# Router logits with stationary router weights in four column groups, and the loop over the later steps written out

## What is computed

```python
def moe(x, sh_gate, sh_up, sh_down, r_gate, r_up, r_down, router_w, router_b):
    shared = expert_ffn(x, sh_gate, sh_up, sh_down)
    logits = x @ router_w + router_b          # (512 tokens, 512 channels) @ (512, 7)
    probs = jax.nn.sigmoid(logits)
    scores, idx = jax.lax.top_k(probs, TOPK)  # TOPK = 2
    ...
```

## Time and profile before

| | us |
|---|---|
| median of 3 runs | 2123.5 |
| lowest and highest | 2117.49, 2135.06 |
| the profiled execution's own time | 2125.45 |
| its span, first to last instruction | 2123.7 |

### The profile page before, as it was taken

How to read it: one execution, slowest core, us unless ns; L and a number is a source line. 1 busy time by engine, 2 the same in 40 slices (tenths; PEclk the granted TensorE clock), 3 DMA queues, 4 the chain that set the end, 5 groups by cost and what they waited for, 6 DMA issues and landing times. The chain is left out here.

```text
span 2123.7 us, 27520 instructions
## 1 busy us (share of the span) xinstructions
PE 1885.2 (89%) x9226; PEld 1238.9 (58%) x9226; DVE 1377.2 (65%) x2196; ACT 994.7 (47%) x1736; POOL 786.7 (37%) x1057
## 2 busy tenths in 40 slices
PE   7878665998999899997999899898899999899895
PEld 3446443695458565695447555496446666588442
DVE  5766698574563799574664699577554499667411
ACT  1412774462322786363232698264142399355021
POOL 1146377441210276561120177372020157472201
PEclk9989755998999999998999999999899999899898
DMA  6337100000213185200213176210022257310683
GB/s 259 109 115 245 52 0 20 1 2 1 99 45 119 57 266 173 96 25 22 79 51 119 35 244 227 84 41 21 17 97 93 69 175 263 127 41 21 237 311 104
DMA packets 55072, 221.09 MB, mean 104 GB/s; under 512 B 6288, under 2 KB 6288, under 8 KB 46992
## 3 DMA queue, kind: packets, MB, share of 16 engines
q1 hardware_dynamic: 45776, 195.14, 26.5%
q0 software_dynamic: 5120, 16.78, 2.4%
q10 hardware_dynamic: 4032, 7.34, 0.9%
HBM read 179.65 MB, written 39.58 MB: 103 GB/s over the span
## 5 line engine op out<-in xcount | busy, mean ns | idle before, releaser
L1933 POOL TENSOR_TENSOR Y<-Y,HC 128x1024 f32<-128x1024 f32 x116 | 273.9, 2362 | 174.0 <-DVE HC L1336 173.4
L1325 DVE TENSOR_TENSOR_SCAN HS<-DA,ps 128x1024 f32<-128x1024 f32 x128 | 292.3, 2284 | 23.5 <-PE ps L742 13.0
L534 PE MATMUL ps<-ring,XNT 128*128 128x512 f32 x384 | 182.4, 633 | 21.0 <-issue 12.2
L1688 ACT ACTIVATE DA<-DL,AB,AN 128x511 f32<-128x511 f32 x256 | 193.8, 806 | 14.8 <-DVE HS L1325 13.5
L954 PE MATMUL ps<-ring,XBT 128*128 128x512 f32 x384 | 188.5, 597 | 0.0
L1801 ACT ACTIVATE PD<-ps,NMX 128x128 f32<-128x128 f32 (+3 forms) x256 | 135.1, 530 | 101.2 <-DVE NMX L1470 99.2
L1470 DVE TENSOR_REDUCE NMX<-ps 128x1 f32<-128x128 f32 (+3 forms) x256 | 124.3, 487 | 65.4 <-PE ps L805 65.1
L823 PE MATMUL ps<-V,PTD 128*128 128x33 f32 x1280 | 164.2, 262 | 0.0
L823 PEld LDWEIGHTS ps<-V,PTD 128*128 128x128 f32 x1280 | 162.6, 192 | 0.5 <-ACT PTD L839 0.5
L650 PE MATMUL ps<-XNH,tern 128*128 128x512 f32 x352 | 139.2, 396 | 9.8 <-DVE tern L1225 5.4
L534 PEld LDWEIGHTS ps<-ring,XNT 128*128 128x128 f32 x384 | 76.6, 204 | 117.4 <-issue 108.1
(11 more groups left out here) (248 smaller groups left out, 4026.0 us busy)
## 6 DMA issues: line engine op xcount, KB each, us to landing
ring<-experts_dram SPq DMA_DIRECT2D x48, 1024.0 KB, 5.1
tern<-tern_q SPq DMA_DIRECT2D x33, 768.0 KB, 4.2
ring<-experts_dram SPq DMA_DIRECT2D x48, 512.0 KB, 5.4
RAW<-tern_dram SPq DMA_DIRECT2D x22, 768.0 KB, 4.8
ring<-wqkv_dram SPq DMA_DIRECT2D x4, 3072.0 KB, 11.9
XB<-xg SPq DMA_DIRECT2D x42, 256.0 KB, 3.6
yg<-YB SPq DMA_DIRECT2D x42, 256.0 KB, 4.9
tern_q<-tern SPq DMA_DIRECT2D x11, 768.0 KB, 7.0
```

The source lines that it names most:

```text
L534: last = pe.matmul(ps[:, 2 + 3 * (i % 2) + part], XNT[:, k, tile(i)], wqkv[:, k, part * C:(part + 1) * C], start=(k == 0), stop=(k == NK - 1))
L1325: v.tensor_tensor_scan(HS[:, q].rearrange("p j t -> p (j t)"), DA[:, q].rearrange("p j t -> p (j t)"), ps[:, 2 * q:2 * q + 2].rearrange("p ...
L1688: s.activation(DA[:, u % 2, jj, 1:T], DL[:, j, 1:T], ACT.Exp, scale=AN[:, j * NS + n:j * NS + n + 1], bias=AB[:, j * NS + n:j * NS + n + 1 ...
L1933: p.tensor_tensor(y, y, HC[:, q], ALU.add).then_inc(c_y, 1)
```

## The change

The router's weights are padded from 8 to 32 columns and become the stationary operand: `pe_logit_parts` issues four products, one for each block of channels k, each with 512 tokens as moving columns, into partitions 32k to 32k + 31 of bank 7 (bank 5 in `finish`). It stands ahead of tile 0 in `pe_A` and ahead of everything in `pe_experts`. ScalarE copies the 128x512 bank to a new tile ZT as its first work of the step (`s_logit_parts`). `pe_logits`, at its old place ahead of tile 1, waits for that copy and issues four products with 128 tokens of ZT stationary and 8 columns of a constant `fold` (four stacked unit matrices) moving, which adds the four parts and turns the result. In `finish` this second product comes behind the four gate products. The loop over steps 1 to 3 becomes three calls of `step` in a row.

```diff
-                  ("wo1", NK * C), ("wr", NK * 8), ("ident", P), ("bdt", NK), ("dpar", NK),
+                  ("wo1", NK * C), ("wr", NK * 32), ("ident", P), ("fold", 8), ("bdt", NK), ("dpar", NK),
...
+    ZT = at("ZT", [P, T], F32, "keep", 24 * KB)
...
         def pe_A(pe, experts):
+            if experts:
+                pe_logit_parts(pe)
             for i in range(NT):
                 if i == 1 and experts:
                     pe_logits(pe)
...
+        def pe_logit_parts(pe):
+
+            for k in range(NK):
+                last = pe.matmul(ps[32 * k:32 * k + 32, r_bank()], wr[:, k], XET[:, k], start=True, stop=True,
+                                 skip_group_check=True)
+            last.then_inc(e_part, 1)
+
         def pe_logits(pe):
-            for i in range(NT):
-                for k in range(NK):
-                    last = pe.matmul(ps[:, r_bank(), 8 * i:8 * i + 8], XET[:, k, tile(i)], wr[:, k],
-                                     start=(k == 0), stop=(k == NK - 1))
+
+            pe.wait_ge(e_parts, 1)
+            for i in range(NT):
+                last = pe.matmul(ps[:, r_bank(), 8 * i:8 * i + 8], ZT[:, tile(i)], cst("fold"), start=True, stop=True)
             last.then_inc(e_logit, 1)
...
         def pe_experts(pe):
+            pe_logit_parts(pe)
+            pe_E_part(pe, 0, 0, 0, NK)
             pe_logits(pe)
-            pe_E_part(pe, 0, 0, 0, NK)
             pe_counts(pe)
...
+        def s_logit_parts(s):
+            s.wait_ge(e_part, 1)
+            s.copy(ZT[:], ps[:, r_bank()]).then_inc(e_parts, 1)
...
         def s_A(s, experts):
+            if experts:
+                s_logit_parts(s)
...
         def s_experts(s):
+            s_logit_parts(s)
             s_route(s)
...
         step(x_rows[1], None, False)
-        with nc.Fori(1, B) as b:
-            step(x_rows[bass.ds(b + 1, 1)].rearrange("o p i c -> (o p) i c"),
-                 out_rows[bass.ds(b - 1, 1)].rearrange("o p i c -> (o p) i c"), True)
+        for b in range(1, B):
+            step(x_rows[b + 1], out_rows[b - 1], True)
         finish()
...
-    pad8 = np.zeros((C, 8), np.float32)
+    pad8 = np.zeros((C, 32), np.float32)
...
+        "fold": np.tile(np.eye(32, 8, dtype=np.float32), (NK, 1)),
```

More of the change, by code:

```diff
@@ L430, in build @@
         e_zb = sem("e_zb")
+        e_part = sem("e_part")
+        e_parts = sem("e_parts")
         e_sig = sem("e_sig")
```

## The result

| | before | after |
|---|---|---|
| median | 2123.88 (20 runs) | 2115.26 (20 runs) |
| lowest and highest | 2116.73, 2135.06 | 2111.37, 2124.07 |
| the profiled execution's own time | 2125.45 | 2111.37 |
| its span | 2123.7 | 2109.2 |
| mean granted clock | 0.928 | 0.932 |

What follows compares the result with a forecast made beforehand. Taken to bound it: the loop's jumps, TensorE's dense products up to the second q/k tile, and half clock. 7.8 + 3.8 + 0.5 + 3.8 + 1.0 = 16.9 us off 2125.45 gave 2108.5, named 2108; range 2101 to 2118.

Steps and rivals of the forecast that it cites:

- within 1%: Whole kernel: the case that the time changes by less than 1%, 21 us; chance 0.76.
- main forecast: Whole kernel: 2108 us, own range 2103 to 2113; chance 0.55.
- narrower column groups: Part products: rival that groups run two at a time (about 2112 us) or one at a time (2118); chance 0.15 for both.
- a clock that falls all the same: Steps: rival that the clock still falls behind the short products and new idle, 2119.5 us; chance 0.1.
- The rows of a step: Start of each step: 2.3 us idle, parts about 1.9, second product 0.9, tile 2 19.6 us after the first part.
- new wait: TensorE before the counts in each step: the wait for the mask, covered before, now open, 1.1 us idle.
- No loop, 7.8 us: Starts of steps 2 and 3 and the last block: less TensorE idle without the loop, 7.8 us gained.
- steps' logits, 3.8 + 0.5 + 3.8 us: Steps 1, 2 and 3: tile 2 starts sooner with the new logits, by 3.8, 0.5 and 3.8 us.
- After the last step, +1.0 us (0 to 1.3): Block after the last step: counts 1.3 us earlier, of which 1.0 us taken as gain.
- the bound 0: Block after the last step: an earlier scatter may land no earlier, sharing queues with the weights; gain 0.
- Straight code fetched late: Inside steps 2 and 3: rival that TensorE waits for instructions, slower from five waits on, six 2131 us; chance 0.05.
- More than that: Whole kernel: rival that half-clock stretches fall well or the clock rises sooner, 22 us or more gained; chance 0.15.

Runs made afterwards that it cites:

- e6: The changed kernel with the four part products accumulated in one column group, so that nothing runs side by side: 2121.76 us, ratio 0.999 to the kernel before.
- e2: The kernel before with its loop written out as separate steps and the old logits kept: 2124.83 us, ratio 1.0005 to the kernel before.
- e8: The changed kernel with the seventh expert's weights in `finish` requested only after the first two gathered row blocks landed: 2112.85 us, ratio 0.9941 to the kernel before.
- r1: The kernel before, unedited, traced a second time: 2119.92 us (one run).
- r2: The same kernel as e2, unedited, traced a second time: 2122.11 us (one run).
- e10: e2 with the old 32 logit records cut into two halves of 16, ahead of tile 1's q and k projections: 2112.33 us, ratio 0.9946 to the kernel before.
- e1: The changed kernel with the loop over steps 1 to 3 put back: 2119.14 us, ratio 0.998 to the kernel before.
- e3: The changed kernel with the counts behind tile 2's q projection, and in `finish` behind four more shared-expert products: 2102.29 us, ratio 0.989 to the kernel before.
- e9: The changed kernel with the edits of e3 and e8 joined: 2101.16 us, ratio 0.9893 to the kernel before.
- e7: The changed kernel with the counts behind tile 2's q projection in the steps only, `finish` left as changed: 2102.94 us, ratio 0.9911 to the kernel before.

## Why the prediction was right or wrong

The forecast was 2108 (2101 to 2118). Measured were 2115.26: within the range, in the case "within 1%", 7 us off the named value. It lies outside the main forecast's own range, 2103 to 2113. The wide range holds it because it was widened for narrower column groups and a clock that falls all the same, and neither came; that it holds is partly luck. The start of a step was foreseen, the sum of the steps was 2.2 us too high, and the block after the last step went the other way.

- *The rows of a step*: right, each within 0.1 us: parts four wide, copy hidden, second product, new wait, idle before the first product, tile 2 at 19.7 behind the first part. The two changes into and out of column groups show no cost beyond 0.1 us: tile 0 ended 521.78 - 511.44 = 10.34 us behind the first part, against 10.26 reckoned without one. The two narrower cases of the column groups did not occur; e6 shows what one group costs.
- *No loop, 7.8 us*, and *steps' logits, 3.8 + 0.5 + 3.8 us*: their sum was too high, since it took the falls of one trace for a property of the kernel, and the two terms cannot be added up in any order. The sum for the three steps was 7.6 + 8.1 = 15.7. The pair of traces used gave 1471.4 - 1454.4 = 17.0, but two traces of before average 1468.0, so the gain is 13.5. "In steps 1 and 3 it fell, in step 2 it did not" was read as a property of the steps; the next trace had one fall in place of two. And the jump's 3.6 us and the fall's 3.4 us are not independent. With the new logits in, the two jumps are worth 1461.6 - 1454.45 = 7.2 us (7.6 forecast), and the logits ahead of them 1468.0 - 1461.6 = 6.4 (8.1 forecast). With the old logits, taking the jumps away is worth 1468.0 - 1465.0 = 3.0 us in the traces and nothing when timed (1.0005, e2), since the fall then comes in every step; the logits are then worth 10.5. So either term can be right, according to which change is taken first, and the loop alone does not pay.
- *After the last step, +1.0 us (0 to 1.3)*: failed, beyond the lower bound. The 1.7 us by which the scatter started sooner were lost before the rows came (33.90 against 33.97 us), as the bound 0 had it. (The prediction has scatter and weights share the queues. The profile counts them on two, q0 with the 16.78 MB of the indirect transfers and q1; what they share is the 16 DMA engines.) And the shared expert's earlier end, which was counted as slack, moved SyncE's request to within 0.4 us of the rows' request. That cost 3.35 us of idle, and `finish` lost 143.4 - 141.7 = 1.7 us in the first pair, 144.15 - 141.4 = 2.75 by the means. The prediction asked what the earlier scatter would collide with and not what the earlier weights would. e8 shows it. Where the two requests do not collide, `finish` takes 141.4 us on average with the old logits (139.8 to 142.8 in before, r1, e2, r2, e10) and 140.6 with the new ones in four groups (139.9 to 142.0 in e1, e3, e8, e9): close to the 1.0 us forecast, but within the spread, so not shown.
- *Own time and span*: every kernel with three steps written out has 2.1 to 2.3 us outside its span, with a loop 1.65 to 1.85; 0.4 us that the prediction did not have.
- By this 13.5 - 2.75 - 0.4 = 10.4 us remain against 8.6 measured. The rest may be the stretch until step 1, which varies by more than that, or the number of falls in the timed runs of before, which only a trace can count; it is not settled.
- *The clock falls all the same* did not come true: none of the nine traces with the new logits has a fall behind them. *Straight code fetched late* did not either. One wait that the profile puts to "issue" does stand in each step, 3.0, 4.0 and 3.1 us long and some 330 us in (L756, `pe_C_out`), and the kernel before has it just so (L751); it ends 0.1 us behind VectorE's last `Y`, for which TensorE waits there by a semaphore. No other wait put to "issue" of over 2 us stands in the three steps. *More than that*, a better clock behind a denser start, did not happen by itself. It did once the new wait was covered (e7): the wait was priced at 1.1 us, and its removal gave 3.5 a step.

## What to carry to other kernels

A stall that sits next to a change of the clock has no price of its own: look at two or three traces of the same kernel, count how often the clock falls there, and try the removal alone before adding it to a sum. A long row of short products need not be made faster: cut in two by dense ones it kept the clock. And when a change makes an engine finish sooner, look up which transfer that engine releases, and what small transfer on the path now stands beside it.

## What the runs showed of the hardware that was not expected

- 32 records of 8 columns in one row, 3.6 to 4.7 us, were followed by half clock in 9 of 12 steps (before, r1, e2, r2), in 8 of 8 entered in a straight line and 1 of 4 entered by a jump; the same records as 16 and 16 with 3.7 us of dense products between were so in none of 3 (e10).
- Four column groups of 32 with 512 moving columns each, float32: 8 records in 1.94 us at half clock, in one group 6.10, most of it at half clock.
- The jump back took TensorE 3.4 to 4.0 us in its compare-and-branch; the other four engines 0.04 to 0.07.
- Two requests on two queues 0.15 to 0.4 us apart were followed by a delay of the smaller of 3.4 to 3.6 us; from 0.64 us apart on no such delay was seen.
- A scatter that started up to 2.9 us sooner (14.4 to 17.4 us behind the first product) was through no sooner: the request behind it stood at 30.9 to 31.6 us in 14 traces. In before and after the DMA engines were full from 4 to 28 us (share 0.99 to 1.04).
